# A second hand-written order of the same instructions for every engine of a sandwich of mixer, attention and FFN

## The chip, the cores and the metric

The kernel runs on one core of one Trainium2 chip. The metric is the device time of one launch in microseconds; with one core, that core's time is the kernel's. Several runs were timed, and one more was taken with the profiler.

## What is computed

The input x has 16 sequences ("units") of 256 tokens by 128 channels. The reference, cut to its stages:

```
x = x + layernorm(block(layernorm(x)))       # mixer, MLP, attention, MLP
x = x + layernorm(ffn(layernorm(x)))
block: n = rms(x);  value, gate = n @ in_proj;  value = silu(causal_conv4(value))
       B, C = x @ B_proj, x @ C_proj          # 16 heads of 64 states
       y = chunked scan(value, B, C) + D*value;  x += (y * silu(gate)) @ out_proj
       x += relu(rms(x) @ m_fc)**2 @ m_proj
       q, k, v = rms(x) @ ...;  rope;  causal softmax attention, 16 heads of 8, 4 kv heads
       x += y @ o_w;  x += relu(rms(x) @ a_fc)**2 @ a_proj
ffn:   h = silu(x@w1)*(x@w2);  h = gelu(h@h1);  h = gelu(h@h2);  h @ w3      # 512 wide, ternary weights with scales
```

## The kernel before

All weights are loaded once and kept in SBUF. Weights and activations of the large products are split into a high and a low part in fp32r, and three matmuls replace one (high by high, high by low, low by high). In the first microseconds the kernel prepares weights: ACT writes the high part, and DVE or POOL the low part. For the decays of the scan ACT writes exponentials into LM (`w_decay`, L687), and POOL masks them (L606). These preparations are the chain W.

A unit passes nine further chains of named steps (`_chains`, L88): N (load and norms), M (turns, gates, convolution), S (the scan: `bc` projects B and C for a pair of heads, `sc` multiplies them, `mask` on DVE applies LM, `va` multiplies with the values, `yg` on DVE and then POOL finishes a half of the output), D (`m_out`, `n2_turn`, `up`, `down`), H and K (queries, keys, score maxima), A (attention: `wts` are the score products whose Exp is taken on ACT, `pv` the product with V), T (output projection, `n4_turn`, `up_b`, `down_b`) and F (`gate`, `hidden1`, `hidden2`, `ffn_out`). Within a chain the order of steps is fixed, unit after unit. How the chains are interleaved is written out by hand, for each engine apart, as a string of chain letters in `TURNS` (L112): the engine takes its next step from the chain that the next letter names. Up to six or seven units are in flight at once. There is no dynamic choice: an engine that waits for a semaphore in one step holds up all that stands behind it in its string.

PSUM has eight banks, and all chains draw on all of them. `BANKS` (L146) lists the bank of each tile in the order in which PE opens the tiles. `_banks` (L195) works out which tile held that bank last, and `wait_free` (L378) makes PE wait until that holder has been evacuated.

`FILL` (L160) names PE's steps before which PE issues dummy matmuls of the identity into the bank that the step will open: the number is the count of calls, and each call of this fp32 product makes two matmul records. The fill first waits for the bank, and the step's own data are waited for behind it:

```
        for c in TURNS[engine]:
            name, i, k = next(chains[c])
            if engine == "PE" and (name, i, k) in FILL:
                parts["fill"](_opened(name, k), i, FILL[name, i, k])
            parts[name](i, k)
```

Steps that matter below: ACT's `w_mix` (L674, the high part of w_mfc), `w_back` (L677) and `w_ffn` (L681); POOL's `w_mix` (L614), `w_back` (L623), `w_ffn` (L631), which work on these, and POOL's `yg` (L524), which multiplies the gate in. PE's `m_out` (L1347) waits for `yg`; `n2_turn` (L1357) waits for the norm that POOL's `m_sq` and ACT's `m_norm` make.

Of the kernel before, what the change touches and what calls it, by code (L numbers as in the profile page):

```python
# [87 lines left out]
def _chains():  # L88
# [24 lines left out]
    PE=("MMMMMMSSSMSSSMSSSSSSSSSSDDMSSSMSSSSSSSDSDDSDDDDHDHDDMMSSDMMSSSDSSMSHSSSSHSMKKMSSSDSMDMSSKDDDSMSDDSSSSSKSHMSMKDMSSMDSSSHS"  # L113
        "SMSADSSSKKAASDDSASDADDDKKADAKDHDAMASSHAAMSSSAKMATAMSSKASMTKAASSTSSAKATSKTASTTAAAATATKDDDDKAAFAKDFFFFHMAKTHASMSDMSFFDKSSM"
        "FFSAAASSAMFFTTSSKSSTTTSKTASKDDAADDAKFAFFFAFMKDSSDMHTFMMFSASHSAAFSMFATTDFFKSSSSKSSTTTSTASKDDAADDKAFAFFMFFAKDSSDTMFSHMFAAH"
        "MSSAFSMFAFFSTSTSSKSSTTSKTDASDDKAATDAFDKAFFFMFAKDSSDHMTFMFSAAADHMSSFSMFASSFFKKTTSSSSTTTSASKDDAATDDAFKAHFFMFFAKDHMSSMMFDFS"
        "TSASFFAASMFASSFDTTSSKTSSTKSASKDAADATKDDFTAFFFFMDKASHSMHDMFFSTSAMAASFSMFSAFKFTSSSDTTSSTSKTASKDDAADTDAKFAFFFFMDKASSHDMFMST"
        "FHSSAAMAFSMFADFSSFKKTSSTTSSTTSTASKDDAADDKFAAFFFFMKDASSDHTMFMHFSAAAMTSSFSMFASTFFSSSSSTKTKDSATSKDDAADTDKFAAFFFFMDAKHSSMDFM"
        "MTHFSAASSFSAFFTAMFSDTSSSSSTTKSTKASKDDAATADDKAFMFFDFFKASSDTSMFMHFHMAASSAFMFSASSFKKTTFDSSSSTTTSTASKDAADDDAFKAFFFFDKAHDDTHF"
        "AFAATTAFFATTFTFKKAATDDAKFAFFFTFKHATHTFFTTTKTFFAAAKKAFFFAKFFFAFTAATTFFTKAKTFFAAAAFAFFTATFFFAFTAATTFFATTAFFFFFTTFFFFTTTFFT"  # L120
        "TFFFFFFFFFFFFFFF"),
# [1513 lines left out]
```

## Time and profile before

| | before |
|---|---|
| median of 3 runs | 1000.96 us (999.48 to 1003.15) |
| the profiled execution's own time | 1003.44 us |
| its span, first to last instruction | 1001.7 us |
| PE busy | 926.0 us of the span |
| mean granted clock of PE | 0.991 |

The profiled execution is 2.5 us over the median and 0.3 us over the slowest of the three runs; 1.7 us of it lie outside the span. Durations below are of this one execution. PE is TensorE's matmuls, PEld its weight loads, ACT ScalarE, DVE VectorE, POOL GpSimd, SP the queue that issues all DMAs. The order in which an engine takes its steps is read off the `TURNS` string, and a time in the profile is put to a step by the tile names in its row.

### The profile page before, as it was taken

The numbers are of one execution on the slowest core, as the hardware profiler recorded it, in microseconds if no ns is written. First come the engines' busy times: TensorE is split into PE (matmuls) and PEld (weight loads), VectorE is DVE, ScalarE is ACT, GpSimd is POOL, SyncE is SP. The second block draws the span as 40 slices with busy tenths as digits, with TensorE's granted clock in tenths as the row PEclk, the third lists the DMA queues.
The fourth block names the chain that finished last, engine by engine and source line by source line (L and its number), as shares of the span: only waits on it lengthen the run. The fifth ranks groups of instructions, "written<-read, shape, count | busy, mean of one in ns | idle before, by whom it ended". The sixth has DMA issues, their size and how long they took to land.

```text
span 1001.7 us, 24912 instructions
## 1 busy us (share of the span) xinstructions
PE 926.0 (92%) x9520; PEld 802.7 (80%) x9520; DVE 668.7 (67%) x1962; ACT 647.6 (65%) x1511; POOL 463.9 (46%) x739
## 2 busy tenths in 40 slices
...
PEclk9999999999999999999999999999999999999999
...
DMA packets 17204, 14.47 MB, mean 14 GB/s; under 512 B 1856, under 2 KB 15552, under 8 KB 16832
## 3 DMA queue, kind: packets, MB, share of 16 engines
...
## 4 chain that ended last, share of the span: by engine, by line
PE 58%; ACT 14%; DVE 11%; POOL 10%; issue 6%; DMA 0%; SPq 0%; POOLq 0%; ACTq 0%; DVEq 0%
PE bank L1239 54%; DVE M L1030 3%; POOL hD_lo L647 3%; POOL P L577 2%; ACT h L890 2%; POOL hD_lo L642 2%; ACT P L857 2%; PE bank L1250 2%; DVE mneg L1148 1%; ACT h L896 1%; DVE cv L1017 1%; POOL w_h_lo L634 1%; ACT junk L698 1%; ACT LM L692 1%; ACT L890 1%
## 5 line engine op out<-in xcount | busy, mean ns | idle before, releaser
L1030 DVE TENSOR_TENSOR M<-bank,LM 128x384 f32<-128x384 f32 x256 | 126.4, 549 | 69.4 <-PE bank L1239 69.3
L1239 PE MATMUL bank<-hD_hi,w_h_hi 128*128 128x256 f32 x512 | 147.7, 288 | 8.9 <-POOL hD_lo L647 6.5
L1239 PE MATMUL bank<-hD_hi,w_h_lo 128*128 128x256 f32 x512 | 143.6, 280 | 0.0
L1239 PE MATMUL bank<-hD_lo,w_h_hi 128*128 128x256 f32 x512 | 143.5, 280 | 0.0
L1148 DVE TENSOR_REDUCE mneg<-bank 128x2 f32<-128x512 f32 (+1 forms) x192 | 122.1, 683 | 13.7 <-PE bank L1239 13.5
L857 ACT ACTIVATE P<-bank 128x512 f32<-128x512 f32 x192 | 102.7, 611 | 18.2 <-PE bank L1239 18.0
L577 POOL TENSOR_SCALAR_AFFINE_SELECT P<-P 128x256 f32<-128x256 f32 (+1 forms) x192 | 91.5, 495 | 36.8 <-ACT P L857 34.1
L1239 PEld LDWEIGHTS bank<-hD_hi,w_h_hi 128*128 128x128 f32 x512 | 96.5, 188 | 13.8 <-POOL hD_lo L647 9.3
L1239 PE MATMUL bank<-BC 64*128 64x256 f32 (+1 forms) x1024 | 101.5, 337 | 4.8 <-ACT BC L705 3.6
L705 ACT ACTIVATE BC<-bank 128x512 f32<-128x512 f32 x128 | 75.3, 606 | 46.3 <-PE bank L1239 43.7
L896 ACT ACTIVATE h<-bank,cols 128x256 f32<-128x256 f32 x128 | 53.4, 471 | 79.3 <-PE bank L1239 78.9
L1239 PEld LDWEIGHTS bank<-BC 64*128 64x128 f32 x1024 | 84.3, 187 | 20.5 <-ACT BC L705 6.2
L1239 PEld LDWEIGHTS bank<-hD_lo,w_h_hi 128*128 128x128 f32 x512 | 96.6, 189 | 0.0
L1239 PEld LDWEIGHTS bank<-hD_hi,w_h_lo 128*128 128x128 f32 x512 | 96.4, 188 | 0.0
L647 POOL TENSOR_TENSOR hD_lo<-h,hD_hi 128x512 fp32r<-128x512 f32 x32 | 40.7, 1291 | 102.8 <-ACT hD_hi L906 102.8
L1239 PE MATMUL bank<-ident 128*128 128x128 f32 x464 | 63.3, 283 | 9.3 <-DMA M<-in_w_in 7.3
L1239 PEld LDWEIGHTS bank<-ident 128*128 128x128 f32 x464 | 57.8, 197 | 11.2 <-issue 7.6
L499 POOL TENSOR_TENSOR oms<-omv,eps_ln 128x2 f32<-128x2 f32 x16 | 3.2, 201 | 114.0 <-DVE omv L977 114.0
L642 POOL TENSOR_TENSOR hD_lo<-h,hD_hi 128x512 fp32r<-128x512 f32 x32 | 40.6, 1284 | 30.5 <-ACT hD_hi L745 30.3
L1239 PE MATMUL bank<-P,Va 128*32 128x256 f32 (+1 forms) x512 | 47.9, 491 | 4.8 <-POOL P L577 4.2
L1017 DVE SCALAR_TENSOR_TENSOR cv<-vpad,cols,cv 128x256 f32<-128x256 f32 x96 | 50.0, 521 | 3.4
L1239 PE MATMUL bank<-M,xpad 128*32 128x128 f32 (+1 forms) x1024 | 48.2, 329 | 4.3 <-DVE M L1030 4.1
...
## 6 DMA issues: line engine op xcount, KB each, us to landing
...
```

Of the source, the lines that this page charges most:

```text
L577: g.affine_select(p3, p3, [[0, parts], [1, P]], ALU.is_ge, zero, base=0, channel_multiplier=-1).then_inc(S["pmask"], 1)
L642: g.tensor_tensor(hD_lo[:, two, :], h[:, two, :], hD_hi[:, two, :].bitcast(F32), ALU.subtract).then_inc(S["hd_lo"], 1)
L647: g.tensor_tensor(hD_lo[:, two, :], h[:, two, :], hD_hi[:, two, :].bitcast(F32), ALU.subtract).then_inc(S["hc_lo"], 1)
L705: a.activation(dst, psum(c, i, n) if src is None else src, ACT.Copy).then_inc(evac(c, n), 1)
L857: a.activation(PT[c][:, j, :], psum("A", i, n), ACT.Exp).then_inc(evac("A", n), 1)
L890: a.activation(h[:, j, :], psum_t("F", i, F_W + j), ACT.Silu, scale=cols[:, C_W1 + j:C_W1 + j + 1]).then_inc(S["silu"], 1)
L896: last = a.activation(h[:, j, :], psum("F", i, n)[:, k * TOK:(k + 1) * TOK], ACT.Gelu, scale=cols[:, c + j:c + j + 1])
L1017: v.scalar_tensor_tensor(cv[:, b, :], vpad[:, b, j:j + L], w(j), cv[:, b, :], ALU.mult, ALU.add).then_inc(S["conv"], 1)
L1030: last = v.tensor_tensor(M[:, k % 2, r, e, :], psum("C", i, 2 * n + e)[:, 0:TRI], LM[:, h + e, :, :].rearrange("p a q -> p (a q)"), ALU.mult)
L1148: v.reduce_max(neg, of, axis=AX.X, negate=True).then_inc(evac("K", n), 1)
L1239: return p.matmul(o, lhsT, rhs, start=start, stop=True, skip_group_check=True)
L1250: last = p.transpose(o[:, k * P:(k + 1) * P], src[:, k, :], ident[:])
```

## The change

The steps, their instructions and their tiles stay. The strings of `TURNS` are replaced for all five engines: PE's step differs at 466 of 976 places, ACT's letter at 454 of 1019, DVE's at 316 of 838, POOL's at 192 of 551, SP's at 26 of 48. Most steps move by a few places. The last 26 steps of PE, from `gate` 0 of unit 14 on, and the last 26 of ACT, 22 of DVE and 41 of POOL stay in their order. `BANKS` is replaced (1207 of 1376 entries differ). `FILL` has other entries: 233 calls in all, where there were 232. Each string's first line, the first line of `BANKS` and all of `FILL` stand here:

```diff
-    PE=("MMMMMMSSSMSSSMSSSSSSSSSSDDMSSSMSSSSSSSDSDDSDDDDHDHDDMMSSDMMSSSDSSMSHSSSSHSMKKMSSSDSMDMSSKDDDSMSDDSSSSSKSHMSMKDMSSMDSSSHS"
+    PE=("MMMMSSSSSMMSSSMMMSSSSSSSSDDSSSMSSSSSSSDSDDSDDDDHHDMDDMSSMMSSSDDMSSSHSSSSHSKKMMSSSDSMDSMDKSDDMSDDSSSSSSKSMSKMSSMMDHDSSSHS"
...
-    Activation=("WNNWMMMMMWWWWWNWNSSMMSSMMSSSSWWWSSMMSSMSSDSDSDDDHDHHDDHNDDMNMSSMSMSMHHMSSHNSSHNMMKKSSMDSSDMDMDDMSSHSHSNNMMMHSSMDSSMDSMSD"
+    Activation=("WNNWMMMMWMWWWWSSWNSMMSNMMSSWWSSWSSMMSSMSDSSDSDDDHDHHDDHNMNDMDSSMMSSMHHMSHSSSNNHMMKKSSMDDSDMMSDDMHSSSHSNMNMMSSDHSSDMMMSSH"
...
-    DVE=("NNWWMMMMWNWNWSMMSSWSMSMSSSSSSSSSDSSSDSSSDDNDNHMMHMMDSSSSNHNSSSKSSMMHSSSDMMDKKKHSSDKSSNSKKNSSKKSMMKKKKKMDSMSSSHKKSSDSHSSH"
+    DVE=("WNNMWMMMWWNWNSSSSMMWMSSSMSSSSDSSSSSSDSSSDDNNDHMHMMMSDSSSNHKSNSSSSMMHSSSDMMDKKKHSSDKNSSSKKNSSKKMSKKMKKKMDSMSSSHKKDSSHSSSH"
...
-    Pool=("NNNNNNWWWWWWSSWDSDDDSHDNNNDDDHANNNSSDDDDHSNNNSDDDDSAASAAAAAADDHNAAANANADDAAAAAAAATAAAASTTATAAAAASAAATHDAANATNANDFFDFFFTF"
+    Pool=("NNNNNNWWWWWSWSWDDDDSSHDNNNDDDHNNNSSDDDDHANNNSSDDDSDASAAAAAAADHNAANAANAADAADDAAAAATAAAASATTTAAASAAAAATDAHNATNAANFFFFDDDAA"
...
-    SP=("NNNNTNNTNNFTNTFFNTNTFFTNNTFNFTNTFNTFFTFTFTTFTFFF"))
+    SP=("NNTNNNNNTTNFTNFNFTNTFNFFTNFTNTNFTNTFTFFTTFTTFFFF"))
...
-BANKS = ("012345670123674015746230146572015746021537412035741023576402735640237561402356140275765314026743510247135047135704136071"
+BANKS = ("012345670123452436701243651270567120561732041652370416253714526371425630714563207145614235071423657024573624572436517345"
...
-FILL = {("gates", 0, 0): 3, ("n3_turn", 0, 0): 9, ("n_turn", 0, 0): 5, ("sc", 0, 0): 19, ("sc", 0, 1): 2,
-        ("sc", 0, 3): 2, ("va", 0, 0): 2, ("val_turn", 0, 0): 17, ("wts", 0, 0): 2, ("xm_turn", 0, 0): 23,
-        ("n2_turn", 1, 0): 2, ("scores", 1, 2): 3, ("wts", 1, 0): 2, ("wts", 1, 1): 6, ("xm_turn", 1, 0): 10,
-        ("bc", 2, 0): 2, ("n_turn", 2, 0): 6, ("sc", 2, 1): 2, ("scores", 2, 0): 2, ("scores", 2, 2): 1,
-        ("up", 2, 0): 4, ("wts", 2, 0): 2, ("wts", 2, 1): 3, ("sc", 3, 3): 3, ("scores", 3, 0): 1,
-        ("pv", 4, 1): 1, ("sc", 4, 1): 2, ("scores", 4, 2): 1, ("wts", 6, 1): 2, ("wts", 7, 1): 2,
-        ("wts", 8, 1): 2, ("pv", 9, 1): 1, ("scores", 9, 2): 2, ("wts", 10, 1): 1, ("wts", 11, 1): 2,
-        ("xm_turn", 11, 0): 2, ("n2_turn", 12, 0): 2, ("n3_turn", 12, 0): 1, ("x2_turn", 12, 0): 5, ("q2_turn", 13, 0): 2,
-        ("gate", 14, 0): 6, ("hidden2", 14, 0): 6, ("n4_turn", 14, 0): 3, ("wts", 14, 2): 1, ("gate", 15, 0): 11,
-        ("hidden1", 15, 0): 12, ("hidden2", 15, 0): 13, ("o_proj", 15, 0): 2, ("scores", 15, 0): 2, ("up_b", 15, 0): 6,
-        ("wts", 15, 1): 5, ("xm_turn", 15, 0): 4}
+FILL = {("bc", 0, 0): 31, ("gates", 0, 0): 4, ("n2_turn", 0, 0): 1, ("n3_turn", 0, 0): 9, ("n_turn", 0, 0): 5,
+        ("o_proj", 0, 0): 2, ("qkv", 0, 0): 2, ("sc", 0, 0): 14, ("sc", 0, 1): 5, ("sc", 0, 3): 2,
+        ("wts", 0, 0): 2, ("wts", 0, 2): 2, ("xm_turn", 0, 0): 28, ("gates", 1, 0): 3, ("pv", 1, 0): 1,
+        ("scores", 1, 2): 2, ("x2_turn", 1, 0): 1, ("n2_turn", 2, 0): 6, ("n_turn", 2, 0): 2, ("scores", 2, 0): 2,
+        ("scores", 2, 2): 1, ("wts", 2, 0): 2, ("wts", 2, 1): 3, ("xm_turn", 2, 0): 6, ("y_rows", 2, 0): 1,
+        ("sc", 3, 3): 2, ("scores", 3, 0): 1, ("bc", 5, 5): 2, ("sc", 5, 1): 2, ("n_turn", 7, 0): 1,
+        ("scores", 7, 2): 1, ("x2_turn", 7, 0): 1, ("gate", 9, 0): 1, ("n2_turn", 12, 0): 1, ("o_proj", 13, 0): 2,
+        ("wts", 13, 0): 2, ("gate", 14, 0): 5, ("hidden2", 14, 0): 8, ("o_proj", 14, 0): 2, ("up_b", 14, 0): 2,
+        ("wts", 14, 1): 6, ("gate", 15, 0): 12, ("hidden1", 15, 0): 15, ("hidden2", 15, 0): 16, ("o_proj", 15, 0): 2,
+        ("scores", 15, 0): 2, ("up_b", 15, 0): 6, ("wts", 15, 1): 2, ("xm_turn", 15, 0): 2}
```

Spelled out, the beginnings are these (the number behind a step is its index, 1: is unit 1). PE before: xm_turn, n_turn, gates0, gates1, val_turn, 1:xm_turn, bc0, bc1, sc0, 1:n_turn, bc2, bc3, sc1, 1:gates0, bc4, bc5, va0, sc2, bc6, bc7, sc3, va1, 1:bc0, 1:bc1, m_out0, m_out1. After: xm_turn, n_turn, gates0, gates1, bc0, bc1, sc0, bc2, bc3, val_turn, 1:xm_turn, sc1, bc4, bc5, 1:n_turn, 1:gates0, 1:gates1, va0, sc2, bc6, bc7, sc3, va1, 1:bc0, 1:bc1, m_out0, m_out1. ACT before, from w_split1: w_decay0, 1, 2, 1:norm_in2, w_decay3, 1:nrm_in, bc0, bc1, val_turn, 1:xm_turn, bc2, bc3, 1:n_turn, 1:gates0, bc4, bc5, bc6, bc7, w_mix, w_back, w_ffn, 1:bc0. After: w_decay0, 1, 2, bc0, bc1, w_decay3, 1:norm_in2, bc2, val_turn, 1:xm_turn, bc3, 1:nrm_in, 1:n_turn, 1:gates0, bc4, bc5, w_mix, w_back, bc6, bc7, w_ffn, 1:bc0. POOL before, behind 1:norm_in2: w_decay0 to 3, w_mix, w_back, yg0, yg1, w_ffn, m_sq. After, behind 1:norm_in2 too: w_decay0 to 3, w_mix, yg0, w_back, yg1, w_ffn, m_sq. DVE takes w_heads before norm_in and norm_in2 of unit 0, where it took it behind them, and mask0 to mask3 before 1:xm_turn, where it took 1:xm_turn and 1:n_turn behind mask0.

## Rows read from the trace of the kernel before

**Rows 1.** The page: span, busy time of the engines, granted clock by slice.

```profile
span 1001.7 us, 24912 instructions
...
PE 926.0 (92%) x9520; PEld 802.7 (80%) x9520; DVE 668.7 (67%) x1962; ACT 647.6 (65%) x1511; POOL 463.9 (46%) x739
...
PEclk9999999999999999999999999999999999999999
```

**Rows 2.** Windows over five stretches: busy us (count) per engine, clock, DMA.

```profile
0.00:75.00 75.00, 56.50 (x518) 51.09 (x518) 34.60 (x92) 40.60 (x83) 39.04 (x51) 0.98 0.27 93
75.00:240.00 165.00, 151.71 (x1638) 125.05 (x1639) 130.68 (x360) 94.39 (x251) 67.84 (x117) 0.98 0.03 7
240.00:820.00 580.00, 554.18 (x5871) 479.13 (x5870) 424.69 (x1238) 405.52 (x958) 274.82 (x448) 1.00 0.03 8
820.00:940.00 120.00, 112.59 (x1083) 98.51 (x1081) 66.48 (x229) 84.42 (x177) 62.86 (x100) 1.00 0.03 9
940.00:1001.70 61.70, 51.04 (x416) 48.91 (x416) 12.29 (x44) 22.71 (x46) 19.31 (x25) 0.97 0.03 7
```

**Rows 3.** The page: the chain that ended last, by engine.

```profile
PE 58%; ACT 14%; DVE 11%; POOL 10%; issue 6%; DMA 0%; SPq 0%; POOLq 0%; ACTq 0%; DVEq 0%
```

**Rows 4.** The same chain between 51 and 77 us: start, us, what.

```profile
51.52 0.60 ACT BC L705
52.12 0.53 ACT w_mfc_hi L675
...
52.78 1.28 POOL w_mpj L612
...
63.26 9.07 POOL w_h_lo L634 x2
...
75.57 6.64 PE bank L1239 x76
```

**Rows 5.** Timeline of ACT, 26 to 53 us: start, us, work, [idle before].

```profile
26.43 6.18 ACT L692 ACTIVATE LM<-sl,qs 128x384 f32<-128x384 f32 x12
...
45.80 1.31 ACT L705 ACTIVATE BC<-bank 128x512 f32<-128x512 f32 x2 [0.17 <-PE bank L1239]
50.81 1.31 ACT L705 ACTIVATE BC<-bank 128x512 f32<-128x512 f32 x2 [3.70 <-PE bank L1239]
```

**Rows 6.** Timeline of POOL, 34 to 53 us.

```profile
34.19 4.26 POOL L609 TENSOR_SCALAR_AFFINE_SELECT LM<-LM 128x1024 f32<-128x1024 f32 x4
...
52.78 1.28 POOL L612 TENSOR_TENSOR w_mpj<-w_mpj,rows 128x512 f32<-128x512 f32 x1 [12.39 <-ACT w_mfc_hi L675]
```

**Rows 7.** Timeline of DVE, 38 to 58 us.

```profile
38.03 1.02 DVE L1030 TENSOR_TENSOR M<-bank,LM 128x384 f32<-128x384 f32 x2 [9.95 <-PE bank L1239]
...
52.13 0.47 DVE L1035 SCALAR_TENSOR_TENSOR val<-val,cols,bank 128x256 f32<-128x256 f32 x1
...
57.02 0.48 DVE L1035 SCALAR_TENSOR_TENSOR val<-val,cols,bank 128x256 f32<-128x256 f32 x1 [1.63 <-PE bank L1239]
```

**Rows 8.** Timeline of PE, places between 18 and 76 us.

```profile
18.51 3.96 PE L1239 MATMUL bank<-ident 128*128 128x128 f32 x34
...
60.26 1.30 PE L1239 MATMUL bank<-w_out,val 128*128 128x128 f32 x8 [1.68 <-POOL val L526]
...
75.09 0.44 PE L1250 MATMUL bank<-ident,nrm 128*128 128x128 f32 x2 [1.18 <-ACT nrm L715]
```

**Rows 9.** Timeline of PE, waits in the middle.

```profile
126.89 0.51 PE L1239 MATMUL bank<-n2T_hi,w_mfc_hi 128*128 128x256 f32 x1 [1.06 <-DVE n2T_lo L1002]
...
203.30 1.60 PE L1239 MATMUL bank<-ident 128*128 128x128 f32 x12 [0.62 <-ACT BC L705]
```

**Rows 10.** Waits of PE by producer: us in total, times, longest.

```profile
PE bank L1239 <- POOL hD_lo L647: 6.5, 12, 1.1
...
PE bank L1239 <- ACT P L857: 2.6, 8, 0.5
```

**Rows 11.** One window at a lower clock, and one matmul group at both clocks (timeline).

```profile
232.00:237.00 5.00, 4.38 (x24) 4.38 (x25) 1.98 (x9) 1.82 (x5) 2.71 (x7) 0.66 0.09 26
...
232.62 3.63 PE L1239 MATMUL bank<-w_mpj,hid 128*128 128x128 f32 x16 [0.80 <-DVE x L1195]
...
402.89 2.05 PE L1239 MATMUL bank<-w_mpj,hid 128*128 128x128 f32 x16 [0.65 <-DVE x L1195]
```

**Rows 12.** Timeline of PE, the last idle turns.

```profile
973.86 2.84 PE L1239 MATMUL bank<-ident 128*128 128x128 f32 x24
977.67 0.39 PE L1239 MATMUL bank<-hD_hi,w_h_hi 128*128 128x256 f32 x1 [0.97 <-POOL hD_lo L642]
...
987.65 0.39 PE L1239 MATMUL bank<-hD_hi,w_h_hi 128*128 128x256 f32 x1 [1.11 <-POOL hD_lo L647]
```

More of the change, by code:

```diff
@@ L112 @@
 TURNS = dict(
-    PE=("MMMMMMSSSMSSSMSSSSSSSSSSDDMSSSMSSSSSSSDSDDSDDDDHDHDDMMSSDMMSSSDSSMSHSSSSHSMKKMSSSDSMDMSSKDDDSMSDDSSSSSKSHMSMKDMSSMDSSSHS"
[L114 to L120, printed above, removed]
-        "TFFFFFFFFFFFFFFF"),
@@ new lines @@
+    Activation=("WNNWMMMMWMWWWWSSWNSMMSNMMSSWWSSWSSMMSSMSDSSDSDDDHDHHDDHNMNDMDSSMMSSMHHMSHSSSNNHMMKKSSMDDSDMMSDDMHSSSHSNMNMMSSDHSSDMMMSSH"
+        "DASAKKDSADAAAAAAAADHDAAADAAHNHMDDANSSHSSMAKAAMAATAMMSKAAAAAMSTAAAATTASSATTAAAATAAAAAAAKKHDAAAFDTHAADFFMFTFNHAFFNTSSDMHMF"
+        "FFFSSTMMFFDAAASSAMAAATKSSTKAAAAHAAAAAHFTDFAFDFMNHFFTFDNSSTMMFDHFFFSASMMAAFFADTAMASSTAKSSTKAAAAAAAAAFTDFAFNFMDFFNDFHTSSTM"
+        "HDHMFFFFAASMSHAMFFMAATSSTSASAKKTDAAAAHAAAAAFDTFNAFFMDFFDFNTHSDDMTSHMFFFFAAHSMMASFFMAATSSTAASSKKAAAATHAAAAAHFDTFAFNMFHDFN"
+        "FDMFTHSSMMFFFFSSMDFFTMAAATSAAATSDASSKKAAAAATAAAAFDHAFDFFNMFDHNFHFMTDMSFTSHAFFFTASSMMMTFAFASAAASTDSSKKAAATAHAAAAAFDTFAFMD"
+        "NFFFDNFHMTDSHSMTFFFHFMSAMASFAMFAASSDTAATSSKTKAAAAHAAAAAFHDTFANFFDFMFDFSNTSMHMTFFFFDMMTASSHAAFFMAASASTSSAKKDAAATAHAAAAAFD"
+        "FADFNFFHMFFNDTDTMSMSHFFTHFFAMMTASSFAFSAAMTSDAASSKKAAAATAAAAADHTFDNMFFAFDFFNTSSFDHMMHTFFFFMHSMSAMAFFAAATASATSSSKKTDAAAAAA"
+        "AAAFDTHFDHFADFFFTFHTHDDFFFFAAATTAAAAFFAAAAKTAAKAAATFHTFHFAFFFHTFHTTFFFFTFFAAAKKAFAAAAAAATFTFAFFFTFTTAAAAFFFFAFFAAAAAAFAT"
+        "AAAATFFTFAFFTFATTAAAFFFFAFFTFTFFTFFFTFTTFFFFFFFFFFFFFFFFFFF"),
```

57 lines of the change are left out of this document (28 added, 29 removed).

## The prediction

> **What bounds the kernel now.** I read the page's busy times first: PE is busy for 926.0 of 1001.7 us, DVE and ACT for two thirds, POOL for less than half [rows 1]. So the limit is PE's stream, and a new order can win only what PE now waits. The windows say where that is [rows 2]. From 0 to 75 us PE is idle for 75.0 - 56.5 = 18.5 us, from 75 to 240 for 13.3, from 240 to 820 for 25.8, from 820 to 940 for 7.4, and from 940 on for 10.7; together 75.7. The dummy matmuls hide more of the same: PE counts them as busy. 34 of them took 3.96 us at the full clock, so one call (two records) is 0.233 us [rows 8]. By the diff, the 232 calls before divide into 83 up to the third `sc` pair of unit 0, 54 from `gate` 0 of unit 14 on, and 95 between; so some 22 us of the middle's time are fill beside its 46.5 us of idle time.
>
> Then the chain that ended last: 58% PE, but 14% ACT, 11% DVE and 10% POOL [rows 3]. A chain that leaves PE for over a third of its length says that the order lets other engines decide. Followed in time, one stretch stands out. From 52.12 us it leaves PE for ACT's w_mfc_hi, goes to POOL's w_mpj at 52.78, stays on POOL through the preparation of weights and both `yg` (the two w_h_lo end at 72.33), and comes back to PE only at 75.57 [rows 4]. Nowhere else does it stay off PE for 23 us.
>
> **The start, up to `n2_turn` of unit 0 (75 us): -4.0 us.** POOL idles for 12.39 us until 52.78, for ACT's w_mfc_hi [rows 6]. ACT was idle itself: `bc` 4 and 5 ended at 47.11, it then waited 3.70 us for PE, took `bc` 6 and 7 at 50.81, and only behind them `w_mix` [rows 5]. The new ACT string has `w_mix` and `w_back` straight behind `bc` 5. They wait for weights that landed long ago. So POOL's w_mpj can begin at about 47.9 instead of 52.78: up to 4.9 us.
>
> It can't use all of it. POOL does the same work up to 72.4, with `yg` 0 now between `w_mix` and `w_back`. Taken at old times: w_mpj and w_mfc_lo end at 50.4; `yg` 0 needs DVE's val, which ends at 52.6 [rows 7], so it ends at 53.3; `w_back` takes 4.3 us, to 57.6; `yg` 1 needs the other val, 57.5, so it ends at 58.3; `w_ffn` begins there and not at 60.8. That is 2.5 us. PE fits: it loses the wait of 1.68 us before `m_out` and arrives at `n2_turn` 1.68 us earlier plus the 1.18 us that it idled there, 2.9 us in all [rows 8].
>
> To win more, the scan of unit 0 must itself come earlier. For: ACT copies bc0 and bc1 straight behind the twelve exponentials (6.18 us, [rows 5]), no longer behind the squares of unit 1, four more exponentials and a norm. w_split1 slips by 0.9 us, as `w_scale` on DVE ends later: DVE's `w_heads` now comes first and puts off the norm, the gates and the convolution of unit 0 by about 1.2 us. Net, `sc0` begins near 34.5, not 36.95. `bc2` and `bc3` follow it on PE at once, so `sc1` comes near 39.9, not 42.5: 2.6 us. Against: POOL's w_decay0 stands behind the norm of unit 1, whose squares ACT now takes near 37. So LM is masked near 39.4 and not at 35.3, and `mask0` starts at 39.5, not at 38.03 [rows 6, 7]: 1.5 us late. DVE has 9.95 us of idle time before it, so nothing else is held up, and mask1 to mask3 follow it without the turns of unit 1 between. The front gains between -2.6 and +1.5 us; I take -1.5, nearer to `sc1`, since four masks in a row catch up the late first one. Sum: -2.5 - 1.5 = -4.0 us, with -4.9 and -1.0 as ends. The fill of 31 calls before bc0 (7.2 us) takes the place of 17 and 10 calls before `val_turn` and 1:xm_turn. It covers the wait for the split weights of B and C, which ends near 28 us in both orders; cost 0.
>
> **The middle, 75 to 940 us: -3.0 us.** The skeleton stays. I added up PE's steps, in the order of either string, with their durations in the trace: the mean step moves by 0.7 us of PE work, the large blocks (`hidden1`, `pv`, `bc`) by almost nothing. Only `up_b` goes far, up to 15 us earlier in five units. What changes is what stands just ahead of a step that waited. `up` of unit 2 idled 1.06 us behind 4 fill calls, with nothing between it and its `n2_turn`; now two `bc` (1.4 us) stand there, but 6 fill calls (1.4 us) have come in ahead of that `n2_turn`. `wts` 1 of unit 1 had 12 dummies (1.60 us) and 0.62 us of idle time [rows 9]; now 1.1 us of work stand ahead, and no fill. PE waited 6.5 us in 12 waits for POOL's hD_lo before `hidden2` [rows 10]; the work between `hidden1` and `hidden2` rises from 3.8 to 4.1 us on the mean. Over the whole middle the diff takes away 60 calls of fill and adds 44, often within a few steps. If each stood for a wait, the gains would be 14.0 us and the losses 10.3: net 16 calls, 3.7 us. I take -3.0, as a call taken away where the wait stays gives nothing. The ends are -14.0 (all relief, no new wait) and +10.3 (new waits alone).
>
> The banks: a step that opens a bank soon after its last holder was written may wait for the reader. With less than 1.2 us of PE work between the two I count 137 of 1376 cases before and 146 after; score tiles (K) rise from 10 to 18 and those of attention (A) from 20 to 32. A wait of this sort is PE for ACT's P: 2.6 us in 8, 0.3 us each [rows 10]. Nine more make 2.9 us at most; they are within the ends above, and I count them as 0 beside the 3.0. SP's order differs in loads and stores that move 128 KB each; DMA is busy for 3% in the middle [rows 2], so 0. If a load came late, norm_in on DVE would wait, a unit ahead of its use.
>
> **The end, from 940 us: 0.** The last 26 steps of PE are the same. More fill stands there, 62 calls for 54, in turns that are idle anyway: before `hidden1` of unit 15 24 dummies ran and PE still idled 0.97 us, before `hidden2` 1.11 us [rows 12]. Three more calls are 0.70 us, under both. If POOL came sooner than now they would cost at most 0.7 each.
>
> **The sum.** 1003.44 - 4.0 - 3.0 = 996.4 us for the profiled execution; the same 7.0 us off the median of the runs give 1000.96 - 7.0 = **994.0 us**. By the ends alone it would be 982 to 1010.
>
> **The clock.** In four short places PE runs at 1.2 GHz, not 2.4: the window from 232 to 237 us shows 0.66 granted. The same sixteen matmuls took 3.63 us there and 2.05 at full clock [rows 11], so one such place costs about 1.6 us. All four follow waits of PE. Which of them the new order keeps I can't tell; two fewer or two more is 3.2 us either way, and I take no change.
> The Trainium skill ("TensorE: Matmul & The Clock Gate", Part 1, "What's actually happening") says that the throttled state is the default and that activity releases it. By that rule fill taken away speaks against this change. The four places here, all behind waits, agree with it.
>
> **The rivals.**
> *The middle pays.* The relieved waits stay relieved, as nothing but PE's stream stands behind them: idle time in the middle falls by a quarter of its 46.5 us. For it: 54% of the chain is PE's matmuls, and the waits are short. Against it: the 44 new calls. Start -4.0, middle -12: 985.
> *The start's gain is given back.* After 75 us units 0 and 1 are still short of work, and PE waits for norms (fill of 9 calls before `n3_turn` 0 in both). If another chain, that of unit 1 or 2, sets the time there, only the last microsecond arrives. Against it: the chain runs through unit 0's POOL work and straight on in PE. 1000 us.
> *Slower: bank and queue misfits.* With 1207 of 1376 banks dealt anew, PE waits for a bank that ACT or DVE has yet to read, and all behind it in PE's string waits too. The place is the K and A tiles. Each such wait is 0.3 to 1.1 us [rows 9, 10]; at 0.6 us, 12 new ones eat the 7.0 us and 20 make it slower by 0.5%. The measure above finds 9 more tight ones, not 20. 1007 us.
> *The clock falls more often.* Fill has gone from turns in the middle, such as the 5 calls before `x2_turn` of unit 12. At 1.6 us each, four more places bring 1000.4. The rule on the page named above would have this happen wherever a wait stays and its fill is gone.
>
> **How the numbers follow.** Forecast 0.48, the middle pays 0.17, given back 0.14, misfits 0.13, clock 0.08. One half of a per cent, 5.0 us, is about what a measurement of this kernel can tell from no change. The forecast's own range is 989 to 999, and it is faster by more than that in four of five cases; "the middle pays" always, "given back" in one of five, the clock in one of four. Faster: 0.38 + 0.17 + 0.03 + 0.02 = 0.60. Slower: 0.09 of the misfits and 0.02 of the others, 0.11. Same: 0.29. The range 984 to 1003 leaves out the best of the second case and most of the misfits, together under 0.2.
>
> **What would show it.** Right: POOL's w_mpj begins near 48 us and `w_ffn` near 57; PE's wait before `m_out` is gone; `n2_turn` of unit 0 starts near 71; from there to the end the span is about 3 us shorter than before (926.6 from 75.1). `mask0` near 39.5. Wrong: `n2_turn` at 71 and the end at 1002 (given back), PE idle over 50 us from 71 to 936 (misfits), more than six places under the full clock.

## The result, and the profile after

The changed kernel takes 1004.21 us (median of 20 executions, 1002.20 to 1008.14), the one before 1001.33 in the same job (997.95 to 1003.15). The ratio over all executions is 1.0037, 95% interval 1.0026 to 1.0049 (the medians alone give 1.0029): slower by a little over a third of a per cent, where 994.0 us was forecast. Its profiled execution has a span of 1005.6 us. First its page, the lines that answer to [rows 1] and [rows 3], and a group of the costliest:

```profile
span 1005.6 us, 24926 instructions
...
PE 925.7 (92%) x9522; PEld 804.0 (80%) x9522; DVE 679.9 (68%) x1962; ACT 648.5 (64%) x1511; POOL 463.9 (46%) x739
...
PE 55%; DVE 16%; ACT 13%; POOL 8%; issue 5%; DMA 0%; SPq 0%; POOLq 0%; ACTq 0%; DVEq 0%
...
L1016 DVE SCALAR_TENSOR_TENSOR cv<-vpad,cols,cv 128x256 f32<-128x256 f32 x96 | 57.1, 595 | 3.4
```

PE is as busy as before, ACT and POOL too. DVE is not: the same 1962 instructions take 679.9 us and not 668.7, and its share of the chain rises from 11% to 16%. The last line shows where 7.1 of the 11 us sit: the 96 steps of the scan's convolution took 521 ns each before (50.0 us together) and take 595 now. An order of work can make the work itself longer.

The windows, as in [rows 2]:

```profile
0.00:75.00 75.00, 58.51 (x537) 53.03 (x538) 35.85 (x92) 39.67 (x80) 37.44 (x48) 0.98 0.28 94
75.00:240.00 165.00, 148.20 (x1635) 122.67 (x1634) 131.52 (x361) 94.17 (x252) 68.15 (x118) 0.99 0.02 6
240.00:820.00 580.00, 547.97 (x5782) 474.19 (x5780) 426.62 (x1222) 402.48 (x948) 273.65 (x449) 0.99 0.03 8
820.00:940.00 120.00, 114.19 (x1110) 99.83 (x1111) 72.19 (x240) 88.05 (x184) 64.32 (x99) 1.00 0.03 7
940.00:1005.60 65.60, 56.82 (x467) 54.32 (x465) 13.72 (x51) 24.16 (x50) 20.33 (x27) 0.98 0.04 11
```

From 75 to 940 us PE now idles 16.8 + 32.0 + 5.8 = 54.6 us and not 46.5; the middle also has 16 calls of fill fewer, some 4 us that PE counted as busy. Windows of equal time hold unequal work, so the next table cuts both traces at the starts of the same steps of PE. The steps are of the unit that the number names, so "bc 2" is the first `bc` of unit 2. Each cell is the stretch's length / PE's idle time in it / time at half clock, in us. The last row ends with PE's last matmul, some 6 us before the span does. The last two columns are kernels from the experiments.

| from step to step | before | after | three_fixes | late_new |
|---|---|---|---|---|
| start to n2_turn 0 | 75.1/18.6/3.4 | 76.6/17.8/3.4 | 75.5/16.0/6.8 | 72.8/16.9/3.4 |
| to bc 2 | 17.9/1.9/0 | 16.3/0.6/0 | 16.3/0.5/0 | 17.8/1.9/0 |
| to m_out 2 | 24.2/0.7/0 | 28.1/3.3/3.4 | 24.9/1.9/0 | 24.3/0.7/0 |
| to m_out 5 | 118.9/10.6/6.6 | 115.2/11.4/0 | 116.4/11.2/3.4 | 115.9/10.6/0 |
| to gate 1 | 63.9/3.6/0.2 | 64.5/3.7/0 | 64.5/3.7/0 | 63.7/3.6/0 |
| to o_proj 4 | 107.4/4.6/0 | 111.3/7.2/3.4 | 108.7/6.2/0 | 107.4/4.5/0 |
| to m_out 10 | 115.4/5.2/3.4 | 115.5/6.9/3.4 | 115.1/6.7/3.4 | 114.8/6.4/0 |
| to hidden2 8 | 195.4/8.2/0 | 194.9/8.3/6.8 | 194.1/8.6/3.4 | 192.9/8.7/0 |
| to hidden2 11 | 146.5/7.3/0 | 147.7/8.7/0 | 147.7/8.7/0 | 147.6/8.3/0 |
| to gate 14 | 77.5/4.5/0 | 76.2/3.7/0 | 76.2/3.7/0 | 76.2/3.7/0 |
| to PE's last matmul | 53.5/4.5/0 | 53.4/2.5/0 | 53.2/2.5/0 | 53.4/2.5/0 |

The change wins 1.6, 3.7 and 1.3 us in three stretches and loses 3.8 and 3.9 in two, each of which has a new half-clock place. Most of the 3.7 is clock too: before's profile has two half-clock places in that stretch, and late_new, with before's order and none of them, takes 115.9 us there, against 115.2 with the changed order.

Four single waits of PE in the middle last 1.9 us or more; before, the longest was 1.24. The timeline of the first, of PE, POOL and DVE in the changed kernel:

```profile
93.84 2.04 POOL L554 TENSOR_TENSOR hid<-hid 128x512 f32<-128x512 f32 x2
...
93.97 0.96 DVE L1092 SCALAR_TENSOR_TENSOR qs<-qs 128x40 f32<-128x40 f32 x1
...
94.97 0.96 DVE L1090 TENSOR_TENSOR qs<-qs 128x40 f32<-128x40 f32 x1
95.97 0.20 DVE L1091 SCALAR_TENSOR_TENSOR qs<-qs 128x40 f32<-128x40 f32 x1
...
97.08 0.41 DVE L1001 TENSOR_TENSOR nT_lo<-bank,nT_hi 128x256 fp32r<-128x256 f32 x1
97.55 0.19 PEld L1238 LDWEIGHTS bank<-nT_hi,w_in_hi 128*128 128x128 f32 x1 [3.12 <-DVE nT_lo L1001]
97.55 0.39 PE L1238 MATMUL bank<-nT_hi,w_in_hi 128*128 128x256 f32 x1 [2.91 <-DVE nT_lo L1001]
```

and of the kernel before, the same place:

```profile
93.19 0.42 DVE L1002 TENSOR_TENSOR nT_lo<-bank,nT_hi 128x256 fp32r<-128x256 f32 x1 [0.99 <-ACT nT_hi L750]
...
93.53 1.03 DVE L1091 TENSOR_TENSOR qs<-qs 128x40 f32<-128x40 f32 x1
...
95.54 0.36 PE L1239 MATMUL bank<-nT_hi,w_in_hi 128*128 128x256 f32 x1
```

DVE's order puts `rope2` of unit 0, eight instructions, ahead of the split that `gates` of unit 2 waits for. PE waits 2.91 us. It would be less if each of the short ones took the 0.20 us of the third DVE line; but POOL squares `hid` at the same time, and those beside it take 0.96. A half-clock place follows, in windows from 92 to 97 and 97 to 102 us (the clock is the third number from the end):

```profile
92.00:97.00 5.00, 2.61 (x19) 2.05 (x18) 4.73 (x10) 2.98 (x7) 3.80 (x5) 1.00 0.00 0
97.00:102.00 5.00, 4.45 (x26) 3.94 (x28) 3.16 (x8) 1.20 (x2) 0.00 (x0) 0.66 0.02 3
```

The other three are of the same sort:

```profile
199.59 2.13 DVE L1016 SCALAR_TENSOR_TENSOR cv<-vpad,cols,cv 128x256 f32<-128x256 f32 x3
...
202.50 2.45 DVE L1016 SCALAR_TENSOR_TENSOR cv<-vpad,cols,cv 128x256 f32<-128x256 f32 x3
...
205.94 0.71 PE L1238 MATMUL bank<-ident 128*128 128x128 f32 x4 [2.61 <-DVE M L1029]
...
398.07 1.02 DVE L1116 CAST Kb<-ro 128x64 bf16<-128x64 f32 x1
...
400.94 0.62 PE L1412 MATMUL bank<-ident_bf,Qb 128*128 128x128 bf16 x8 [1.91 <-DVE Kb L1121]
...
489.81 3.32 DVE L1016 SCALAR_TENSOR_TENSOR cv<-vpad,cols,cv 128x256 f32<-128x256 f32 x3
...
490.06 2.79 POOL L646 TENSOR_TENSOR hD_lo<-h,hD_hi 128x512 fp32r<-128x512 f32 x2 [5.30 <-ACT hD_hi L905]
...
493.06 1.01 DVE L1029 TENSOR_TENSOR M<-bank,LM 128x384 f32<-128x384 f32 x2
...
494.21 0.54 PE L1249 MATMUL bank<-ident,bn 128*128 128x128 f32 x2 [2.10 <-DVE M L1029]
```

At 205.9 us the fill before the sixth `bc` of unit 5 waits 2.61 us for its bank. `BANKS` gave it the bank of a score tile of the same unit, which `mask` has yet to read, and `mask` stands behind two convolutions of 2.13 and 2.45 us, where 1.5 is usual. The stretch as a whole has only 0.8 us more idle time than before's, since shorter waits and fill are gone; I left this place alone in all experiments. At 400.9 us `qk_turn` of unit 6 waits 1.91 us for Kb, whose splits stand behind the norm of unit 2, two masks and a `yg`; one of the splits took 1.02 us, where 0.19 is usual. At 494.2 `n4_turn` of unit 5 waits 2.10 us for a bank: it was given that of a score tile of unit 10, whose reader `mask` (it writes M) stands behind a convolution of 3.32 us, with POOL's hD_lo beside it.

### The profile page after: what moved, and what is told of

It reads as the page before. It is cut to its first block, busy times and chain, and to the rows that moved or that the text cites. A ratio compares the mean times of both kernels' runs of the same rounds, so it can differ in the third digit from the quotient of the medians.

```text
span 1005.6 us, 24926 instructions
## 1 busy us (share of the span) xinstructions
PE 925.7 (92%) x9522; PEld 804.0 (80%) x9522; DVE 679.9 (68%) x1962; ACT 648.5 (64%) x1511; POOL 463.9 (46%) x739
## 3 DMA queue, kind: packets, MB, share of 16 engines
q8 instruction: 77, 1.26, 0.5%
## 4 chain that ended last, share of the span: by engine, by line
PE 55%; DVE 16%; ACT 13%; POOL 8%; issue 5%; DMA 0%; SPq 0%; POOLq 0%; ACTq 0%; DVEq 0%
PE bank L1238 51%; DVE M L1029 3%; DVE cv L1016 2%; POOL P L576 2%; DVE mneg L1147 2%; ACT h L889 2%; ACT P L856 2%; POOL hD_lo L646 2%; PE bank L1249 1%; ACT junk L697 1%; POOL hD_lo L641 1%; POOL w_h_lo L633 1%; PE bank L1454 1%; ACT LM L691 1%; ACT L889 1%
## 5 line engine op out<-in xcount | busy, mean ns | idle before, releaser
L704 ACT ACTIVATE BC<-bank 128x512 f32<-128x512 f32 x128 | 75.5, 603 | 54.3 <-PE bank L1238 51.4
L1238 PE MATMUL bank<-ident 128*128 128x128 f32 x466 | 63.9, 285 | 12.2 <-DMA M<-in_w_in 8.1
L1016 DVE SCALAR_TENSOR_TENSOR cv<-vpad,cols,cv 128x256 f32<-128x256 f32 x96 | 57.1, 595 | 3.4
L587 POOL TENSOR_TENSOR bhid<-bhid 128x512 f32<-128x512 f32 x32 | 33.4, 1052 | 48.1 <-ACT bhid L880 48.1
```

The lines of the kernel that those rows point to most:

```text
L587: g.tensor_tensor(two, two, two, ALU.mult).then_inc(S["hid_b"], 1)
L704: a.activation(dst, psum(c, i, n) if src is None else src, ACT.Copy).then_inc(evac(c, n), 1)
L1016: v.scalar_tensor_tensor(cv[:, b, :], vpad[:, b, j:j + L], w(j), cv[:, b, :], ALU.mult, ALU.add).then_inc(S["conv"], 1)
L1238: return p.matmul(o, lhsT, rhs, start=start, stop=True, skip_group_check=True)
```

## The experiments

Every execution comes with its span and its mean granted clock, so that a difference in time can be split into what the clock makes and what it doesn't. I fitted the spans of all 20 kernels here with a constant for each kernel and one slope for all. The span grows by 751 us for each 1.0 of clock lost (7.5 us for each 0.01), and what is left over scatters by 0.9 us. "Equal clock" is a kernel's constant less before's 993.8 us: what the waits and the work make. "Clock" is 751 times its mean loss of clock, less before's (1 - 0.9937) * 751 = 4.7 us. The first has a standard error of 0.2 to 0.5 us, the second of 0.2 to 0.9, and of 1.1 for new_to_515. Before has 118 executions with spans, of which the 107 with times of their own are in the fit (with all 118 no figure of the table moves by more than 0.1 us), mean span 998.6; the changed kernel has 20, mean 1003.0. This is a difference of 4.4 us, where the job of the result, whose runs of before have no spans on record, gives 3.8. The profiled executions of both lay some 3 us above these means.

| kernel | median us | ratio, 95% interval | equal clock | clock |
|---|---|---|---|---|
| changed | 1004.21 | 1.0037 [1.0026, 1.0049] | +1.7 | +2.7 |
| start_new | 999.64 | 0.9995 [0.9983, 1.0008] | 0.0 | -0.6 |
| start_old | 1003.59 | 1.0030 [1.0016, 1.0044] | +1.2 | +2.0 |
| heads_back | 1003.65 | 1.0045 [1.0029, 1.0062] | +2.0 | +2.1 |
| prep_early | 995.87 | 0.9958 [0.9945, 0.9972] | -2.4 | -1.9 |
| new_to_150 | 1006.11 | 1.0069 [1.0049, 1.0088] | +4.4 | +1.5 |
| new_to_300 | 1002.57 | 1.0030 [1.0017, 1.0043] | +2.6 | -0.5 |
| new_to_515 | 1009.58 | 1.0110 [1.0091, 1.0129] | +7.9 | +1.7 |
| fill_old | 1011.54 | 1.0121 [1.0101, 1.0140] | +4.3 | +6.8 |
| turn_first | 1003.32 | 1.0025 [1.0010, 1.0040] | +0.8 | +1.7 |
| rope_first | 1002.80 | 1.0025 [1.0010, 1.0039] | +1.3 | +1.0 |
| three_fixes | 1000.62 | 1.0003 [0.9990, 1.0016] | -1.6 | +2.0 |
| combo | 996.66 | 0.9964 [0.9951, 0.9977] | -4.2 | +0.9 |
| less_fill | 1001.48 | 1.0007 [0.9996, 1.0019] | +0.8 | +0.3 |
| more_fill | 1004.75 | 1.0055 [1.0036, 1.0074] | +2.9 | +2.0 |
| four_fixes | 1005.84 | 1.0058 [1.0042, 1.0073] | +2.1 | +3.4 |
| late_new | 994.89 | 0.9952 [0.9935, 0.9969] | -3.4 | -1.6 |
| conv_behind | 998.02 | 0.9973 [0.9957, 0.9989] | -0.4 | -1.7 |
| best_of | 994.71 | 0.9951 [0.9932, 0.9971] | -4.1 | -0.4 |

### Which half: start or rest

The strings can be cut where both orders have issued the same steps. The diff, in words: all five strings, the banks and the fill from one kernel up to 85 us, from the other behind it.

```diff
 start_new:  changed up to 85 us | before from there
 start_old:  before up to 85 us  | changed from there
```

> The changed kernel up to n3_turn of unit 0, the kernel before from there on. Theory 1: +1.6 us, ratio 1.0016. Theory 2: +3.7 us, 1.0037. If the new start were as good as forecast, -4 us, 0.996.

> Strings, banks and fill of the kernel before up to n3_turn of unit 0 (85 us), those of the changed kernel from there on. Theory 1, the loss of 3.7 us is made in two places, some 1.6 us before 85 us and the rest behind it: ratio to before 1.001 to 1.004 (+1 to +4 us). Theory 2, all the loss comes from the start, and what follows is as good as before: 1.000, within 1 us.

Both theories put a loss into the start, and start_new shows none: the changed start is worth nothing and costs nothing. The loss is behind 85 us, 1.2 us at equal clock and 2.0 in clock.

```diff
 heads_back (changed kernel, DVE)
-w_heads norm_in norm_in2 xm_turn
+norm_in norm_in2 w_heads xm_turn
```

> The changed kernel with one edit: DVE takes w_heads behind norm_in2 of unit 0 and not ahead of norm_in. Theory 1, the gates of unit 0 come 2.5 us late for this, and the exponentials of LM and the first mask with them: gates of unit 0 near 17 us, first mask near 39.5 and not 40.5, total 1 to 2 us less than the changed kernel (ratio to before 1.002). Rival, the 31 fill calls ahead of bc and DVE's later wait for LM hide it: no change against the changed kernel (1.0037).

Within its error this is the changed kernel; the rival is right. `w_heads` ahead of the first norm, which the prediction counted among the costs of the front, isn't the cause.

```diff
 prep_early (kernel before)
-ACT:  bc5 bc6 bc7 w_mix w_back w_ffn      POOL: w_mix w_back yg0
+ACT:  bc5 w_mix w_back bc6 bc7 w_ffn      POOL: w_mix yg0 w_back
```

> The kernel before with one part of the change: ACT takes w_mix and w_back ahead of bc 6 and 7 of unit 0, and POOL takes yg 0 ahead of w_back. As forecast, POOL's chain starts 4.9 us earlier and 2.5 us of it arrive: n2_turn of unit 0 near 72.6 us, total -2.5 us, ratio 0.9975. Rival, the convolution on DVE is stretched where POOL now works beside it (0.49 to 1.38 us each, as in the changed kernel at 53 us), mask 7 and va 1 come later: n2_turn near 74 to 75, total within 1 us of before.

4.2 us faster by the medians, from two moves: 2.4 at equal clock, where 2.5 was expected, and the rest clock. The convolution was stretched once, to 2.51 us, and cost nothing that the time shows. Its trace has no wait before `m_out`, and `n2_turn` comes at 72.14 and not 75.09:

```profile
47.34 1.27 POOL L603 TENSOR_TENSOR w_mpj<-w_mpj,rows 128x512 f32<-128x512 f32 x1 [5.89 <-ACT w_mfc_hi L666]
...
57.98 1.05 PE L1230 MATMUL bank<-w_out,val 128*128 128x128 f32 x8
...
72.14 0.44 PE L1241 MATMUL bank<-ident,nrm 128*128 128x128 f32 x2 [0.76 <-ACT nrm L706]
```

So the mechanism of the forecast's first step exists. The changed start holds the same two moves and loses what they win elsewhere (conv_behind, and the last part).

### Where behind 85 us: cuts that mislead

```diff
 new_to_150, new_to_300, new_to_515: changed up to that time | before from there
```

> Kernel: orders, banks and fill of the changed kernel up to about 150 us of the span, those of the kernel before from there. The new start alone, up to 85 us, gave 0.9995 of the time before; the new rest alone 1.003. Theory 'lost at once' (the changed kernel is 4.0 us late at 117 to 127 us of its own profile, as VectorE's scan steps of units 2 to 4 run beside GpSimd's work, and what is lost there is never recovered): 1003 to 1004 us. Rival 'lost behind' (the delay of that stretch is absorbed by the waits up to 240 us, where the changed kernel's profile is level with before's, and the loss comes from the steady part between 300 and 530 us): 999.5 to 1000.5 us.

> Kernel: the changed kernel's orders, banks and fill up to about 300 us, those of before from there. Theory 'lost at once': 1003 to 1004 us, as with the cut at 150 us. Rival 'lost behind': 999.5 to 1001 us, since the changed kernel's profile is only 0 to 1.4 us late between 240 and 300 us.

> Kernel: the changed kernel's orders, banks and fill up to about 515 us, those of before from there. Theory 'lost at once': 1003 to 1004 us again. Rival 'lost behind': 1003 to 1005 us, a step of 3 us or more over the cut at 300 us, since the profile of the changed kernel goes from 1.4 us late at 300 us to 5 or 6 us late at 400 to 530 us.

Neither theory fits: two of the three are slower than the changed kernel itself. Their traces show why. A seam joins two orders that were not made for each other, and makes its own wait: 2.9 us before `sc` of unit 4 (for DVE's xm) at 153.8 us, and 2.4 us before the last `sc` of unit 10 at 517 us. Only up to the seam do such kernels tell something: all three have the wait for nT_lo, and their half-clock place at 95 to 96 us.

### Fill

```diff
 fill_old:  changed order, before's fill everywhere
 less_fill: before's order, the changed fill from 300 us on (19 calls up to 900 us, not 33)
 more_fill: changed order, before's fill from 300 us on
```

> Kernel: the changed kernel's orders and banks, but before's idle turns filled, with before's counts (232 filling products instead of 233; the same steps have them as before). Theory 'orders': the loss is in the orders, so the time stays at 1003 to 1005 us. Rival 'clock' (the fill that was taken from the waits before wts of units 1, 6, 7, 8, 10 and 11 lets TensorE's clock fall more often: six stretches of 3.4 us at half clock before the last 10 us in the changed kernel's profile, four in before's): 1000.5 to 1002 us, and two stretches fewer.

> Kernel: the kernel before, orders and banks untouched, with the changed kernel's filling products at the steps from 300 us on (19 instead of 33 up to 900 us; 89 instead of 97 in all from 300 us). A filling product counts twice (two matmuls of about 0.12 us). Theory 'fill': the fill behind 300 us costs time where TensorE wouldn't have been idle, and holds the clock: the span at equal clock falls by 1 to 3 us and the mean granted clock falls from 0.994 to 0.991 or less, so that the time stays within 1.5 us of before: 999 to 1001.5 us. Rival 'order': the clock stays at 0.994 (then the changed kernel's lower clock is made by its order) and the time falls to 997.5 to 999 us.

> Kernel: the changed kernel, orders and banks untouched, with before's filling products at the steps from 300 us on. Theory 'fill': mean granted clock up from 0.990 to 0.993 or more, span at equal clock 1 to 3 us longer, time 1003 to 1005 us. Rival 'order': the clock stays at 0.990 and the time grows to 1005 to 1007 us.

Both sides of fill_old missed by far. Fill belongs to its order: before's in the changed start stands ahead of steps that no longer wait, `sc1` comes 5 us later, and PE spends 17.1 us at half clock before `n2_turn` 0, for 3.4 before. But behind 300 us fill hardly matters. In less_fill the stretch from `m_out` 10 to `hidden2` 8 stays at 195.3 us while its idle time rises from 8.2 to 10.5: a call taken away left its wait behind. The two times fell into the ranges of theory "fill", but not for its reason: the clock term moved by 0.3 us (less_fill, from before) and -0.7 (more_fill, from the changed kernel, with an error of 0.5). So fill behind 300 us doesn't make the lower clock. Fill between 85 and 300 us was not varied by itself.

### The three waits

```diff
 turn_first (changed kernel, DVE)          rope_first (kernel before, DVE)
-xm_turn2 rope2/0 n_turn2                 -xm_turn2 n_turn2 rope2/0
+xm_turn2 n_turn2 rope2/0                 +xm_turn2 rope2/0 n_turn2
```

> Kernel: the changed kernel with one pair of VectorE steps swapped back: n_turn of unit 2 (the split of nT that gates of unit 2 wait for) runs ahead of rope2 of unit 0, as in the kernel before, instead of behind it. Theory 'queue behind stretched work': in the changed kernel's profile TensorE waits 2.9 us at 97.55 us for nT_lo, which stands behind 10 short VectorE instructions of rope2, some of them 0.78 to 0.96 us long instead of 0.20 while GpSimd squares hid beside them; right behind the wait comes a stretch of 3.4 us at half clock (98.4 us). With the swap the wait falls below 0.6 us and that stretch goes: 2.5 to 4 us less, 1000 to 1001.7 us. Rival 'no single place': the time was lost by many small delays, and what is saved at one place is waited for at the next: 1003 to 1004.5 us.

> Kernel: the kernel before with the same pair swapped the other way and nothing else: rope2 of unit 0 ahead of n_turn of unit 2. Theory 'queue behind stretched work': nT_lo comes 3 to 4 us later (97 instead of 93.6), down of unit 1 covers 1.1 us of it, gates of unit 2 wait about 1.5 us; with a half-clock stretch behind it 1.5 to 3.5 us slower, 1001.5 to 1003.5 us. Rival 'no single place': 999.5 to 1000.5 us, as before.

One swap, both ways. Taken out, it wins 0.9 us at equal clock; put into the kernel before, it costs 1.3 there and 2.5 us by the medians (1002.80 against 1000.31). In turn_first's profile the split ends at 93.7 us and the half-clock place at 98 is gone, but the next step waits in its turn:

```profile
97.51 1.58 PE L1230 MATMUL bank<-BC 64*128 64x256 f32 x16 [1.56 <-issue]
```

PE's idle time up to `m_out` 2 falls from 3.3 to 2.0 us, so of 2.9 us less than half comes back. Both theories had a part: the place is real, and smaller than its wait.

```diff
 three_fixes (changed kernel, DVE): turn_first, and
-f_stats2 f_norm2 mask8/4 yg8 mask8/5 split16/6     -conv10/0 mask10/0
+split16/6 f_stats2 f_norm2 mask8/4 yg8 mask8/5     +mask10/0 conv10/0
```

> Kernel: the changed kernel with three VectorE steps put earlier: n_turn of unit 2 as above; split16 of unit 6 ahead of f_stats of unit 2 (in the changed kernel's profile qk_turn of unit 6 waits 1.9 us at 400.9 us for Kb, whose splits stand behind mask and last 0.7 to 1.0 us instead of 0.2 beside GpSimd's squares; as in before it stands ahead of f_stats); mask 0 of unit 10 ahead of conv 0 of unit 10 (n4_turn of unit 5 waits 2.1 us at 494.2 us for a bank that mask reads, behind a scan convolution that lasts 3.3 us instead of 1.5 beside GpSimd's hD_lo). Each of the three waits is followed by a stretch at half clock. Theory 'queue behind stretched work': the three waits go, some 6 us of idle time, and one to three stretches of 1.7 us with them, less what the next waits take back: 995 to 999 us. Rival 'no single place': 1002 to 1004 us.

3.3 us less than the changed kernel at equal clock, 3.6 by the medians: as fast as before, and between the two ranges. At equal clock it is 1.6 us better than before. What keeps it level is the clock, whose term went from +2.7 to +2.0, a change that its error of 0.6 doesn't tell from none.

```diff
 four_fixes (three_fixes, DVE)
-rope1/8 rope2/8 mrow7 mask10/0 conv10/0 conv10/1
+conv10/0 conv10/1 rope1/8 rope2/8 mrow7 mask10/0
```

> Kernel: the changed kernel with the three VectorE steps put earlier, and a fourth: both scan convolutions of unit 10 ahead of rope1 and rope2 of unit 8, so that they run some 4 us before GpSimd's hd_part of unit 5 and not beside it. With three steps moved, sc of unit 10 waits 2.0 us at 495 us. Theory 'contention': the convolution of unit 10 lasts 0.49 us a step instead of up to 1.39 (3 us less on VectorE), the wait at 495 us falls below 0.6 us: 998.5 to 1000 us, the span at equal clock 1 to 2 us below that of three_fixes. Rival 'the work just takes that long there' (the rope steps that now run beside GpSimd are stretched instead, and the wait moves): 1000 to 1001.5 us.

5.2 us slower than three_fixes. The convolution is cured, and what now stands beside POOL's hD_lo is stretched instead:

```profile
480.81 1.53 DVE L1008 SCALAR_TENSOR_TENSOR cv<-vpad,cols,cv 128x256 f32<-128x256 f32 x3
...
485.37 2.50 POOL L638 TENSOR_TENSOR hD_lo<-h,hD_hi 128x512 fp32r<-128x512 f32 x2 [5.34 <-ACT hD_hi L897]
...
485.55 1.15 DVE L1077 SCALAR_TENSOR_TENSOR qs<-qs 128x40 f32<-128x40 f32 x1
486.74 1.19 DVE L1078 SCALAR_TENSOR_TENSOR qs<-qs,yi 128x40 f32<-128x40 f32 x1
...
490.22 0.21 DVE L1145 TENSOR_TENSOR Qs<-mneg,Qs 128x32 fp32r<-128x32 f32 x1
```

Qs, for `q2_turn` of unit 7, is written 6.5 us later than in three_fixes (483.69): 0.8 of older delay, 3.8 of convolutions and 1.9 of stretch. PE waits 5.1 us for it. The convolution's length went as theory "contention" had it, the rival is right about the move, and the loss is larger than either expected.

### Why the changed start gains nothing, and what adds up

```diff
 conv_behind (start_new, DVE)
-conv1/0 mask0/4 yg0 mask0/5 conv1/1 mask0/6 mask0/7
+conv1/0 mask0/4 yg0 mask0/5 mask0/6 mask0/7 conv1/1
```

> Kernel: start_new (the changed order up to 85 us, before's from there; 0.9995) with one VectorE step put later: conv 1 of unit 1 behind mask 7 of unit 0. In start_new's profile this convolution lasts 3.4 us beside GpSimd's w_back (1.5 in before), the masks 6 and 7 stand behind it and TensorE waits 3.6 us for them ahead of va 1 of unit 0 (1.7 in before). Theory 'queue behind stretched work': the wait falls to about 2.1 us (sc 3, which the masks read, ends some 1.5 us before the convolution does), the span at equal clock is 1 to 2 us shorter, time 997.8 to 998.8 us. Rival 'GpSimd's chain binds' (w_ffn, which n2_turn of unit 0 waits for, starts no earlier): 999.3 to 1000 us.

The changed kernel's start, and conv_behind's, at the step `va` 1 of unit 0:

```profile
52.68 1.33 POOL L611 TENSOR_TENSOR w_apj<-w_apj,bhid 128x512 f32<-128x512 f32 x1
...
52.91 3.38 DVE L1016 SCALAR_TENSOR_TENSOR cv<-vpad,cols,cv 128x256 f32<-128x256 f32 x3
...
58.21 2.79 PE L1238 MATMUL bank<-M,xpad 128*32 128x256 f32 x32 [3.60 <-DVE M L1029]
```

```profile
55.21 1.51 PE L1230 MATMUL bank<-M,xpad 128*32 128x256 f32 x32 [1.50 <-DVE M L1021]
...
56.13 1.52 DVE L1008 SCALAR_TENSOR_TENSOR cv<-vpad,cols,cv 128x256 f32<-128x256 f32 x3
```

The wait falls from 3.60 to 1.50 us, the thirty-two matmuls run at full clock, and `n2_turn` comes at 73.16 us, in start_new at 75.91. The time falls by 1.6 us (medians, against start_new), but at equal clock only by 0.4, with an error of 0.4. In the profile the gain of 2.7 us at `n2_turn` is 1.2 at `bc` 2 and nothing at `m_out` 5, with half-clock places at 73.9 and 230.9 us. So the trace shows the place, and the times don't show that it costs anything at equal clock.

```diff
 combo:    prep_early up to 85 us | three_fixes
 late_new: prep_early up to 515 us | changed
 best_of:  prep_early to 85 | turn_first to 300 | before to 515 | changed
```

> Kernel: up to about 85 us the kernel before with its weights' split moved ahead (w_mix and w_back of ScalarE ahead of the last two bc of unit 0, yg of unit 0 ahead of w_back on GpSimd: alone 0.9958 of the time before), from there the changed kernel's orders, banks and fill with the three VectorE steps of the run before this one put earlier. If the two add up: 4 us less than before at the start, and the rest 2 to 4 us better than the changed kernel's rest (which alone gave 1003.6 us): 993 to 997 us. If the rest's loss isn't in these three waits: 999 to 1001 us.

> Kernel: up to about 515 us the kernel before with its weights' split moved ahead (0.9958 alone), from there the changed kernel as it is. In the profiles the stretch from 523 to 718 us takes 192 to 195 us in the changed order against 195.4 in before's, that from 718 to 865 us 1.2 us more and that from 865 to 942 us 1.2 us less. If the late part of the change is a gain by itself: 992.5 to 995 us. If what it gains goes to the clock or to the seam between the two orders: 995.5 to 999 us.

> Kernel: up to about 85 us before's order with the weights' split moved ahead; from 85 to 300 us the changed order with n_turn of unit 2 ahead of rope2 of unit 0; from 300 to 515 us before's order; from 515 us the changed order. Each piece alone: start 4 us; 85 to 300 us at equal clock about 1 us better than before; behind 515 us at equal clock about 1 us. If they add up and the two seams cost nothing: 992.5 to 994.5 us. If a seam costs what the one at 515 us cost in new_to_515 (5 us) or the clock takes it: 996 to 1000 us.

All three are faster than before, by 0.4 to 0.5%, and faster than the changed kernel by more. combo and late_new lie in the ranges for pieces that add up, best_of 0.2 us above its own. best_of, late_new and prep_early can't be told apart by their intervals. At equal clock best_of is 4.1 us under before, 0.7 more than late_new; its clock takes that back. late_new is 1.0 us under prep_early at equal clock, with an error of 0.6, and its clock term of -1.6 is that of prep_early (-1.9).

## Why the prediction was wrong

**The start, -4.0 us.** Of its two terms the first (-2.5) was right in mechanism and size: prep_early, which is that step alone, measured -2.4 us at equal clock. The second, the front (-1.5), failed. `sc0` came 1.1 us earlier and `sc1` 0.8 (forecast 2.5 and 2.6), `mask0` at 40.52 and not 39.5. And the sum stopped at `sc1`: `n_turn` and both `gates` of unit 1 now stand between `sc1` and `sc2` on PE, where only `gates` 0 stood, and from `sc0` to the last `sc` it takes 17.2 us, in start_new too, for 15.2 before. The last two `sc` come 0.9 us later than before. Then comes a cost of the move itself, which was no term of the sum, as I took DVE's work at its old durations: POOL's w_back, moved forward, runs beside DVE's convolution, which lasts 3.38 us where it lasted 1.53; masks, `va` 1, val, `yg` 1 and `w_ffn` come after it one by one. So w_mpj starts at 49.27 us (forecast 48) and PE's wait before `m_out` is gone, but `w_ffn` starts at 62.32 and not 57, and `n2_turn` at 76.64, not 71. By the times the whole start is worth 0.0 us at equal clock (start_new); how that divides between the front and the convolution isn't shown.

**The middle, -3.0 us.** This step had the wrong sign: start_old, which is the changed rest alone, is 3.6 us slower by the medians, 1.2 at equal clock. Its count of fill was no measure: I priced a call taken away as a wait relieved, and in less_fill 14 calls go up to 900 us and the waits stay. What I looked at on PE's side (work ahead of a waiting step, banks soon reused) missed that four steps had their producer, or their bank's reader, put behind other work on DVE. Three of the four cost 3.3 us at equal clock (three_fixes). The relief that I forecast does exist late in the middle: from `m_out` 10 to `hidden2` 8 late_new takes 192.9 us, before 195.4, both at full clock. PE's work without the dummies takes 183.2 us in both. The dummies fall from 11 calls to 2, and idle time grows by only 0.5 us, where in less_fill, with before's order and the same 2 calls, it grew by 2.3. Waits and dummies before `xm_turn`, `wts` and `n3_turn` together fall from 5.9 to 0.4 us there; before `bc` and `n2_turn` they grow by 1.7.

**Banks, 0.** Two bank misfits are there, of 2.6 us at 206 and 2.1 us at 494. The rival "misfits" had put its place at the tiles K and A and its price at 0.3 to 1.1 us each; both were tiles C, which the rival doesn't name, and their reader was late. Its sign, idle time over 50 us in the middle, came true with 54.6.

**The clock, 0.** This term is larger than the loss at equal clock: +2.7 us for 1.7. The sign of that rival, more than six places, just missed: counted as the prediction counted four before (without the last one, at the span's end), the changed kernel's profile has six. Its mechanism didn't hold behind 300 us: fill isn't what lowers the clock there (less_fill, more_fill). The three moves left the term at +2.0, though each of their waits was followed by a half-clock place in the profile. start_old has it (+2.0), start_new not (-0.6), and late_new, which has the changed order behind 515 us alone, not either (-1.6), so it belongs to the order between 85 and 515 us. new_to_300, which has the changed order up to 300 us, shows none of it (-0.5, error 0.6), which points behind 300 us, but a seam can hide it. Which of the steps there lower the clock is open. The wait at 206 us is taken out by no run: twelve of the profiles here have it, and seven of them show a half-clock place right behind it. The same kernel's executions differ among themselves by as much (the changed kernel's from 0.988 to 0.992), and one profile can't name the place.

**The end and SP, 0.** The end was right: 53.5 and 53.4 us from `gate` 14 to PE's last matmul. Nothing in the runs points at SP; it was not tested by itself.

So the loss is waits behind DVE steps, in part stretched, and a lower clock, while the start's gain of 2.4 us was used up inside the changed start. I had counted the rivals "misfits" (0.13) and "clock" (0.08) as exclusive; they came together. That the time still came within 4 us of before is owed to gains and losses that cancel.
